# Stacked queries ahead of the first cross attention: twelve SBUF copies of one computed tile in place of a second set of matmuls

## The reference, cut to what matters

```python
qkv = x @ w_qkv + b_qkv
q, k, v = jnp.split(qkv, 3, axis=-1)
sa = mha(q, k, v) @ w_so + b_so
x = layer_norm(x + sa, ln_g, ln_b)
qc = x @ w_q + b_q            # the queries that the change is about
kc = y @ w_k + b_k            # y: the context, 16 x 1500 x 96
vc = y @ w_v + b_v
ca = mha(qc, kc, vc) @ w_co + b_co
x = layer_norm(x + ca, ln_g, ln_b)
...
x = layer_norm(x + ff, ln_g, ln_b)
...
```

## Time and profile before

| | us |
|---|---|
| three runs | 1124.32, 1126.2, 1128.36 |
| median | 1126.2 |
| span of the profiled execution | 1126.9 |
| PE busy in it | 1046.1 |
| DVE, ACT, POOL busy | 759.8, 574.5, 389.9 |
| block 3, from its first matmul to its last DVE instruction's end | 69.39 to 98.96 |
| block 4, its first matmul | 99.43 |
| first real scores of block 4 | 119.48 |

### The profile page before, as it was taken

How to read it: one execution, slowest core, us unless ns; L and a number is a source line. 1 busy time by engine, 2 the same in 40 slices (tenths; PEclk the granted TensorE clock), 3 DMA queues, 4 the chain that set the end, 5 groups by cost and what they waited for, 6 DMA issues and landing times. The chain is left out here.

```text
span 1126.9 us, 31634 instructions
## 1 busy us (share of the span) xinstructions
PE 1046.1 (93%) x12060; PEld 741.3 (66%) x12060; DVE 759.8 (67%) x1409; ACT 574.5 (51%) x1139; POOL 389.9 (35%) x273
## 2 busy tenths in 40 slices
PE   4977899999999998979596999999999999999997
PEld 2552566666666665655433777777777777777786
DVE  3646777888788878520575677667767777767652
ACT  2533567777677676642243444544444344444442
POOL 4822012111211112111102554545545555555542
PEclk8977889999999999979898999999999999999998
DMA  3501434344544443030002111111111110111100
GB/s 106 138 2 53 143 117 140 121 130 141 143 131 128 129 142 106 2 97 1 1 22 57 52 55 40 40 53 55 53 55 43 45 53 23 52 53 55 34 4 3
DMA packets 48462, 79.41 MB, mean 70 GB/s; under 512 B 8803, under 2 KB 35253, under 8 KB 48405
## 3 DMA queue, kind: packets, MB, share of 16 engines
q1 hardware_dynamic: 48404, 78.61, 23.1%
HBM read 51.13 MB, written 21.96 MB: 65 GB/s over the span
## 5 line engine op out<-in xcount | busy, mean ns | idle before, releaser
L1374 ACT ACTIVATE P<-PS 125x448 f32<-125x448 f32 x384 | 206.7, 543 | 270.7 <-PE PS L1283 268.7
L1264 POOL TENSOR_TENSOR Pl<-P 125x896 f16<-125x896 f32 x128 | 229.9, 1801 | 242.3 <-ACT P L1374 242.3
L1012 DVE TENSOR_REDUCE m<-PS 128x1 f32<-128x500 f32 x336 | 220.6, 674 | 120.2 <-PE PS L1003 118.4
L918 DVE TENSOR_REDUCE m_part<-PS 128x1 f32<-128x500 f32 x336 | 212.6, 674 | 59.6 <-PE PS L821 58.3
L896 ACT ACTIVATE Pb<-PS 125x448 f32<-125x448 f32 x384 | 187.9, 545 | 36.8 <-PE PS L796 36.1
L1299 PE MATMUL PS<-cNh,P 125*128 125x97 f16 x1344 | 198.1, 208 | 0.1
L1301 PE MATMUL PS<-cNh,Pl 125*128 125x97 f16 x1344 | 197.4, 207 | 0.0
L1300 PE MATMUL PS<-cNl,P 125*128 125x96 f16 x1344 | 196.9, 206 | 0.0
L1300 PEld LDWEIGHTS PS<-cNl,P 125*128 125x128 bf16 x1344 | 131.9, 98 | 25.5 <-issue 0.2
L1299 PEld LDWEIGHTS PS<-cNh,P 125*128 125x128 bf16 x1344 | 131.2, 98 | 15.8 <-issue 3.2
L1281 PE MATMUL PS<-Qh,cTh 110*125 110x448 f16 x384 | 139.0, 362 | 1.3 <-DVE Qh L1450 1.3
(11 more groups left out here) (170 smaller groups left out, 1555.5 us busy)
## 6 DMA issues: line engine op xcount, KB each, us to landing
Kst<-k_halves SPq DMA_DIRECT2D x144, 125.0 KB, 2.7
k_halves<-KH SPq DMA_DIRECT2D x16, 750.0 KB, 3.3
cx<-in_ctx SPq DMA_DIRECT2D x16, 562.5 KB
d_cx<-in_ctx SPq DMA_DIRECT2D x16, 562.5 KB
c_halves<-cHi SPq DMA_DIRECT2D x16, 281.2 KB, 2.7
c_halves<-cLo SPq DMA_DIRECT2D x16, 281.2 KB, 3.0
cTh<-c_halves SPq DMA_DIRECT2D x16, 281.2 KB, 2.9
cTl<-c_halves SPq DMA_DIRECT2D x16, 281.2 KB, 3.6
```

What stands on the lines that cost most here:

```text
L918: nc.vector.tensor_reduce(m_part[:, t, part:part + 1], PS[:, 6 + k % 2, 0:SP], AX.X, ALU.max).then_inc(s_reduced, 1)
L1012: nc.vector.tensor_reduce(m21[:, t, part:part + 1], PS[:, S1[k % 2], 0:SP], AX.X, ALU.max).then_inc(n_red, 1)
L1264: nc.gpsimd.tensor_tensor(Pl[:, c % NP], P1[:, c % NP], high, ALU.subtract).then_inc(n_low_p, 1)
L1374: nc.scalar.activation(P1[:, c % NP, half * HALF:(half + 1) * HALF], PS[0:KC, u % 3, 0:HALF], ACT.Exp).then_inc(n_exp, 1)
```

## The change

`wq3` and `bq3` go, with the six DMAs that loaded them. The queries are computed once, by the matmul that makes `Qall` (L704). ACT rounds it as before; DVE makes `Qrest`, the rest of all 128 rows, in one instruction. SP then issues twelve DMAs from SBUF to SBUF: four from `Qall` to the first block of 32 partitions of `Q16`, four to the second, and, behind a wait for `Qrest`, four from `Qrest` to the third. POOL waits for all twelve (`q_in`) at the start of block 4, before its first `Qst`. The three pieces of context use banks 4, 5 and 2, so none waits for another.

```diff
-        LOOP, ONE, OPEN = range(3)
+        LOOP, BESIDE_Q, OPEN = range(3)
...
-            return WB if mode == ONE else banks[k]
+            return (4, 5, 2)[k] if mode == BESIDE_Q else banks[k]
...
-            elif mode == ONE:
-                pe.wait_ge(ct_split, n * 3 + k)
-            elif mode == OPEN:
+            elif mode != LOOP:
                 pass
...
-        LATER = 25
+        LATER = 19
...
-                for rep in range(3):
-                    sp.dma_start(wq3[:, :, rep, :], w_q.rearrange("d (g r) -> d g r", g=G)).then_inc(later_in, 16)
-                    sp.dma_start(bq3[32 * rep:32 * rep + 32, :], b_q.rearrange("(g r) -> r g", g=G), allow_slow_non_contiguous=True).then_inc(later_in, 16)
...
+            @block.sync
+            def _(sp):
+                sp.wait_ge(a_high, 1)
+                for block_row in range(2):
+                    for g in range(G):
+                        sp.dma_start(Q16[32 * block_row:32 * block_row + 32, g, :], Qall[32 * g:32 * g + 32, :]).then_inc(q_in, 16)
+                sp.wait_ge(a_low, 1)
+                for g in range(G):
+                    sp.dma_start(Q16[64:96, g, :], Qrest[32 * g:32 * g + 32, :]).then_inc(q_in, 16)
...
-                pe.wait_ge(v_kept, 3)
-                for g in range(G):
-                    if g == 2:
-                        pe.wait_ge(a_all_kept, 1)
-                    if g == 3:
-                        pe.wait_ge(a_low, 1)
-                    for half in range(2):
-                        mm = pe.matmul(PS[0:96, A_BANK[g] + half, 0:HALF], wq3[:, g].rearrange("p a b -> p (a b)"),
-                                       T128[:, half * HALF:(half + 1) * HALF], start=True, stop=True)
-                    mm.then_inc(a_q, 1)
-                    if g < NSP:
-                        turn_context(pe, -1, 1, g, mode=ONE)
+                for k in range(NSP):
+                    turn_context(pe, -1, 1, k, mode=BESIDE_Q)
...
-                for g in range(G):
-                    dve.wait_ge(a_high, g + 1)
-                    nc.vector.scalar_tensor_tensor(out=Q16[64:96, g, :].rearrange("p (h c) -> p h c", h=2),
...
-                    if g < NSP:
-                        split_context(dve, -1, 1, g, mode=ONE)
+                dve.wait_ge(a_high, 1)
+                nc.vector.scalar_tensor_tensor(out=Qrest[:].rearrange("p (h c) -> p h c", h=2), in0=PS[:, 6:8, 0:HALF], scalar=bq[:, 0:1],
+                                               in1=Qall[:].rearrange("p (h c) -> p h c", h=2), op0=ALU.add, op1=ALU.subtract).then_inc(a_low, 1)
+                for k in range(NSP):
+                    split_context(dve, -1, 1, k, mode=BESIDE_Q)
...
-                for g in range(G):
-                    act.wait_ge(a_q, g + 1)
-                    nc.scalar.activation(Q16[:, g, :].rearrange("p (h c) -> p h c", h=2), PS[0:96, A_BANK[g]:A_BANK[g] + 2, 0:HALF],
-                                         ACT.Identity, bias=bq3[:, g:g + 1]).then_inc(a_high, 1)
-                    if g < NSP:
-                        keep_context(act, -1, 1, g, mode=ONE)
+                for k in range(NSP):
+                    keep_context(act, -1, 1, k, mode=BESIDE_Q)
...
                         wait_for(pool, st_done, b * NC * 2)
+                        if isinstance(i, int) and i < 0:
+                            pool.wait_ge(q_in, 16 * 3 * G)
```

More of the change, by code:

```diff
@@ L146, in program @@
         b2s = sb("b2s", [128, 4])
-        wq3 = sb("wq3", [D, G, 3, 32])
-        bq3 = sb("bq3", [96, G])
         wq = sb("wq", [D, D])
@@ L153, in program @@
         Qall = sb("Qall", [D, TOK], F16)
+        Qrest = sb("Qrest", [D, TOK], F16)
         Q16 = sb("Q16", [96, G, TOK], F16)
@@ L685, in program @@
         a_proj, a_link, a_var, a_root = sem("a_proj"), sem("a_link"), sem("a_var"), sem("a_root")
-        a_normed, a_turned, a_kept, a_kept_act, a_all, a_all_kept, a_q, a_high, a_low = (
-            sem(n) for n in ("a_normed", "a_turned", "a_kept", "a_kept_act", "a_all", "a_all_kept", "a_q", "a_high", "a_low"))
-        A_BANK = (0, 2, 6, 0)
+        a_normed, a_turned, a_kept, a_kept_act, a_all, a_high, a_low, q_in = (
+            sem(n) for n in ("a_normed", "a_turned", "a_kept", "a_kept_act", "a_all", "a_high", "a_low", "q_in"))
         with nc.Block() as block:
+            @block.sync
[7 more added lines that the diff above has]
+                    sp.dma_start(Q16[64:96, g, :], Qrest[32 * g:32 * g + 32, :]).then_inc(q_in, 16)
             @block.gpsimd
             def _(pool):
-                pool.wait_ge(a_all_kept, 1)
+                pool.wait_ge(a_high, 1)
                 lay_queries(pool, -1, 0)
@@ L724, in _ @@
                 keep_turned_dve(dve, a_turned, a_kept, 0)
-                for g in range(G):
-                    dve.wait_ge(a_high, g + 1)
-                    nc.vector.scalar_tensor_tensor(out=Q16[64:96, g, :].rearrange("p (h c) -> p h c", h=2),
-                                                   in0=PS[64:96, A_BANK[g]:A_BANK[g] + 2, 0:HALF],
-                                                   scalar=bq3[64:96, g:g + 1], in1=Q16[64:96, g, :].rearrange("p (h c) -> p h c", h=2),
-                                                   op0=ALU.add, op1=ALU.subtract).then_inc(a_low, 1)
-                    if g < NSP:
-                        split_context(dve, -1, 1, g, mode=ONE)
+                dve.wait_ge(a_high, 1)
[3 more added lines that the diff above has]
+                    split_context(dve, -1, 1, k, mode=BESIDE_Q)
             @block.scalar
@@ L740, in _ @@
                 act.wait_ge(a_all, 1)
-                nc.scalar.activation(Qall[:].rearrange("p (h c) -> p h c", h=2), PS[:, 6:8, 0:HALF], ACT.Identity, bias=bq[:, 0:1]).then_inc(a_all_kept, 1)
-                for g in range(G):
-                    act.wait_ge(a_q, g + 1)
-                    nc.scalar.activation(Q16[:, g, :].rearrange("p (h c) -> p h c", h=2), PS[0:96, A_BANK[g]:A_BANK[g] + 2, 0:HALF],
-                                         ACT.Identity, bias=bq3[:, g:g + 1]).then_inc(a_high, 1)
-                    if g < NSP:
-                        keep_context(act, -1, 1, g, mode=ONE)
+                nc.scalar.activation(Qall[:].rearrange("p (h c) -> p h c", h=2), PS[:, 6:8, 0:HALF], ACT.Identity, bias=bq[:, 0:1]).then_inc(a_high, 1)
+                for k in range(NSP):
+                    keep_context(act, -1, 1, k, mode=BESIDE_Q)
         with nc.Block() as block:
```

## The result

The changed kernel takes 1123.81 us (median, 1120.81 to 1126.02) where the kernel before takes 1126.33 beside it: a ratio of 0.9975, interval 0.9964 to 0.9987, or 2.8 us less (1.5 to 4.1). Measured once more among the experiments it was 0.9979 (0.9965 to 0.9993). The ratio is taken over the runs of both kernels of one set; the two medians as they stand are 2.5 us apart. So it is faster, but by about half of the 5.7 us forecast.

A forecast was written before the change was run, and what follows sets the result against it. PE is busy 93%, but block 3 ends in a hand-over chain; with SP last at 93.25 plus 0.47, block 4 starts at 93.72 for 99.43, gaining 5.7 us: 1121.2, as median 1120.5, range 1117.5 to 1124.5.

The forecast's parts named there:

- The mechanism: In block 3 SP's twelve issues reach the barrier last, at 93.25, behind DVE's 90.9; everything after moves 5.7 us earlier.
- The pitch of the issues: In block 3 SP issues twelve copies at 0.46 us each, 5.5 us in all; bounds 4.0 and 7.9.
- The barrier behind SP: Block 4's first matmul comes 0.47 us behind the last engine, at 93.72 in place of 99.43.
- The stretch of before: Block 3 from Qall at 87.70: PE, ACT, DVE hand-overs of 11.26 us, then block 4's first matmul at 99.43.
- The step from the trace to the median: Whole kernel: profiled 1126.9 less 5.7 is 1121.2; the runs' median lies 0.7 below that execution, so 1120.5.
- (a): Rival: one slow issue on SP in block 3, 0.6 to 1.3 us above the median: 1121.8; chance 0.12.
- the dear pitch: Second case of (a), in block 3: dearest regular issues, 0.66 us each as for scattered loads: 1122.9.
- (b): Rival: PE's clock comes back late in block 4, costing 0.9 and 1.2 us: 1122.6; chance 0.10.
- (c): Rival: one POOL and DVE collision more in the bodies, 1125.5, chance 0.10; or one fewer, 1115.5, chance 0.07.
- (d): Rival: two more POOL and DVE collisions, in two cross attention bodies, making it slower: 1130.5; chance 0.04.
- (e): Rival: block 3's end is set elsewhere, so the change doesn't do what it says: 1126; chance 0.01.
- The range: Whole kernel: 1117.5 to 1124.5 us, taking in the issue's bounds (1118.9 to 1122.9) and the spread of runs.

The follow-up runs named there:

- The probe: Changed kernel with seven more kinds of DMA on SP in block 3, behind the twelve copies, to time each issue; 1154.13 us as a whole.
- two queues: Changed kernel with the four copies of Qrest issued by ACT, beside SP's eight; 1120.66 us, ratio 0.9969 to the kernel before.
- halves: Changed kernel with each copy cut into two of 448 columns, 24 DMAs, the same bytes; 1130.53 us, ratio 1.0057 to the kernel before.
- the copies moved: Changed kernel with SP issuing its twelve copies at the start of block 4; 1119.33 us (0.9958 to before), again 1117.61 (0.9932).

## Why the prediction was half right

**The mechanism** was right. All engines but SP are through within 3 us of `Qall` (DVE 2.92 forecast 3.2), SP comes last, block 4 starts behind it, and the stretch to the scores is 20.11 where 20.05 was forecast. POOL started `Qst` at 95.11, 1.45 us behind SP's last issue and 0.6 us into block 4 (forecast 1.4 to 3.4), with no one waiting. Three things were mis-sized, all in one direction.

**The pitch of the issues** is the step that failed most. The sum took `Kst`'s 0.46 as nearest, because it too writes 32 partitions. The probe shows that the height has no part in it and that both ends in SBUF have, and no row of before has that. The measured 0.63 lies inside the bounds (0.33 to 0.66), close to the dear end that the prediction gave to scattered loads. Twelve times: 7.61 us in place of 5.55, so 2.1 us of the forecast gain.

**The barrier behind SP.** The 0.47 was read where DVE came last. Behind SP's last issue it is 94.52 - 93.66 = 0.86 here; 0.84 with two queues and with halves. With the copies moved, where DVE comes last again, it is 91.23 - 90.76 = 0.47. So 0.4 us more. The prediction had named this as a sign of being wrong: a block 4 start further from SP's end than half a microsecond.

**The stretch of before** was read from one execution, with PE at 1.2 GHz through the first group of queries. 11.73 against a mean of 10.80 over four: 0.9 us. The hand-overs between PE and ACT hung on that clock, SP's issues did not, so the trace overstated what they could be exchanged for. The prediction did look at the clock, but only behind the barrier, as something that the change might disturb, and not in the stretch that it removed.

Together: 5.7 - 2.1 - 0.4 - 0.9 = 2.3, the difference of the stretches. The sum closes by itself, since its terms are read from the same traces; what is independent of them is the measured 2.8 and 2.4, and they agree.

**The step from the trace to the median** was wrong too. I set the span (1126.9) against the runs (median 1126.2) as if they were the same quantity. Executions with both numbers show the run mostly 1.8 us above its span (1124.49 and 1122.6, 1125.53 and 1123.7, 1126.12 and 1124.3), in a few up to 3.2. If that holds for it, the traced execution was near 1128.7, at the top of before's runs (1124.29 to 1128.66 in thirteen). That was the sign that its stretches might be long. The predicted time was taken off the median, so it did not suffer from this itself.

**The rivals.** (a), one slow issue, did not come: the longest copy took 0.631. But its second case, the dear pitch, is nearly what happened: it named 1122.9. (b), the clock coming back late, did not come in the changed kernel: low again from 109, full from 119, the same order of stretches. It was seen in the second trace with the copies moved, where the stretch to the scores is 20.67 for the 20.11 of the changed kernel: 0.6 us, not 0.9. (c) and (d), collisions of POOL and DVE, kept their places: the same two bodies lose the race by 0.04 us, the first as follows (compare), the other at 439.99 with 4.40 us (446.27 and 4.40 before):

```profile
136.46 2.11 POOL L760 TENSOR_TENSOR Qst<-Q,tab 96x224 f16<-96x224 f16 x4 [24.07 <-PE PS L784]
136.50 2.10 DVE L943 TENSOR_SCALAR mneg<-mhigh 128x7 f32<-128x7 f16 x1
...
138.72 0.28 PE L828 MATMUL PS<-tab,mneg 128*14 128x128 f32 x1 [1.82 <-DVE mneg L944]
```

(e) is out. The range held the time and the chances had the sign right. But the time, 0.25% less, fell above the 1119 to 1122.5 that had 0.56, and inside "within 0.3%", which had 0.20. That chance was too low because the range of the issue term, whose dear end alone gives 3.3 us, was treated as an edge and not as one of two clusters of rows.

**What stays open.** Why `Qall` itself is ready anywhere from 85.9 to 87.8, and why the time behind the first scores varies between 1003.9 and 1007.4 in these traces. Both happen in all kernels and were not tried. Whether the removed loads of block 2 do anything was not tried apart; the range of `Qall` overlaps between the kernels. And why the copies behind the barrier, with the same stretch in both traces, gained 1.9 us over the changed kernel in one set and 5 in the other.

## What to carry to other kernels

Before work is handed to DMAs, count the issues on the queue that must make them and ask what that queue meets next: at a barrier the issue counts, not the transfer, and moving twelve issues across it (3.4 for 8.5 us) shortened the stretch by 5.1 us, more than the 2.3 of the change itself; in time it was 5 us in one set and only 1.9 in the other. Take the price of an issue from a row with the same source and target kinds, not the same shape; where none exists, give the dear cluster of rows a chance of its own and not the edge of a range. Read a stretch that is to be removed from several traces where PE's clock takes part in it, and look first at which place in the runs the traced execution has.

## What the runs showed of the hardware

An issue on SP with both ends in SBUF takes 0.59 us (0.63 from one to the next), independent of bytes (rows of 224 to 1792) and of partitions (16 to 128, the 128 seen once, at 0.54). With one end in device memory the probe's plain copies took 0.30 to 0.46, but scattered loads 0.618. Copies of 56 KB within SBUF landed 2.0 us after their issue, halves of them 1.8. SP and ACT issue side by side almost without loss (8 in 5.29 us for 5.06). Where SP's list with its DMA issues ended last, block 4's first matmul came 0.84 to 0.86 us behind its last issue; where DVE's list ended last, 0.47 behind its last instruction. In one block the clock of PE, 0.50 or 1.00 through one group of four matmul instructions, moved a hand-over chain of 10.3 us by up to 1.5 us from one execution to the next. A DVE instruction of 0.17 us that started 0.04 us behind POOL took 2.10 us, until the last of four POOL instructions in a row, and 4.40 where a fifth of 2.33 followed.
